# Gathered rows in a ring of eight slots, added in pairs on VectorE

## What is computed

```python
def _L0_rec_ref(user_rep, indices, item_embeddings, W_fuse, b_fuse, W_proj, b_proj):
    retrieved = jnp.mean(item_embeddings[indices], axis=1)
    fused_input = jnp.concatenate([user_rep, retrieved], axis=1)
    fused_rep = fused_input @ W_fuse + b_fuse
    logits = fused_rep @ W_proj + b_proj
    return logits
```

## Time and profile before

| what | value |
|---|---|
| median of 3 runs | 384.41 us (383.92 to 385.25) |
| profiled execution, span from first to last instruction | 381.9 us |
| PE busy | 334.2 us, 88% |
| DVE busy | 164.6 us, 43% |
| ACT busy | 75.0 us, 20% |
| POOL busy | 119.1 us, 31% |
| moved by DMA | 79.97 MB, 209 GB/s over the span |
| granted TensorE clock, mean | 0.945 of full speed |

### The profile page before, as it was taken

How to read it: one execution, slowest core, us unless ns; L and a number is a source line. 1 busy time by engine, 2 the same in 40 slices (tenths; PEclk the granted TensorE clock), 3 DMA queues, 4 the chain that set the end, 5 groups by cost and what they waited for, 6 DMA issues and landing times.

```text
span 381.9 us, 5012 instructions
## 1 busy us (share of the span) xinstructions
PE 334.2 (88%) x1420; PEld 263.3 (69%) x1420; DVE 164.6 (43%) x334; ACT 75.0 (20%) x134; POOL 119.1 (31%) x99
## 2 busy tenths in 40 slices
PE   2579069868997998399999999999999999999996
PEld 2233056545885886188888888888888888888885
DVE  3682236436724321424444445454535454545322
ACT  2220026332400200025123121122121212210000
POOL 2877878787878887200000000000000000000000
PEclk9999559968999899689999999999999999999999
DMA  7898899999999999944687767676666767642222
GB/s 237 234 171 154 172 380 270 262 233 369 264 255 224 232 183 203 214 181 154 195 246 226 228 212 217 212 213 202 217 204 215 220 210 218 211 161 88 100 88 99
DMA packets 44208, 79.97 MB, mean 209 GB/s; under 512 B 5913, under 2 KB 33697, under 8 KB 44194
## 3 DMA queue, kind: packets, MB, share of 16 engines
q1 hardware_dynamic: 32370, 56.74, 45.7%
q0 software_dynamic: 10240, 20.98, 28.8%
q10 hardware_dynamic: 1584, 2.10, 1.6%
HBM read 54.19 MB, written 25.60 MB: 209 GB/s over the span
## 4 chain that ended last, share of the span: by engine, by line
PE 57%; POOL 17%; DMA 13%; issue 10%; POOLq 1%; DVE 1%; DVEq 0%
PE bank L645 55%; POOL acc L302 17%; DMA acc<-L_rec_item_embeddings,rows 7%; DMA acc<-L_rec_item_embeddings,lap_rows 4%; DMA idx<-r_indices 1%; PE bank L632 1%; POOLq L323 1%; POOLq L72 0%; PE bank L622 0%; POOL lap_rows L329 0%; DVE acc L493 0%; DVE out_sb L507 0%; POOLq L324 0%; DVE out_sb L450 0%; DVE out_sb L452 0%
## 5 line engine op out<-in xcount | busy, mean ns | idle before, releaser
L645 PE MATMUL bank<-w_hi,f_hi 128*128 (+1 forms) x400 | 159.7, 399 | 6.3 <-DVE out_sb L507 6.3
L645 PE MATMUL bank<-w_lo,f_hi 128*128 (+1 forms) x400 | 158.1, 395 | 0.0
L645 PE MATMUL bank<-w_hi,f_lo 128*128 (+1 forms) x400 | 157.5, 394 | 0.0
L507 DVE TENSOR_TENSOR out_sb<-bank,early 128x500 f32<-128x500 f32 x100 | 67.8, 678 | 146.0 <-PE bank L645 117.5
L645 PEld LDWEIGHTS bank<-w_hi,f_hi 128*128 128x128 f32 x400 | 76.8, 192 | 27.7 <-DVE out_sb L507 7.2
L348 ACT CAST w_hi<-w_raw 128x500 f32 (+1 forms) x100 | 59.5, 610 | 145.4 <-DMA w_raw<-L_rec_W_proj 135.8
L645 PEld LDWEIGHTS bank<-w_hi,f_lo 128*128 128x128 f32 x400 | 76.8, 192 | 16.0
L645 PEld LDWEIGHTS bank<-w_lo,f_hi 128*128 128x128 f32 x400 | 76.9, 192 | 15.0
L425 DVE TENSOR_TENSOR w_lo<-w_raw,w_hi 128x500 fp32r<-128x500 f32 (+1 forms) x100 | 66.3, 672 | 21.4 <-ACT w_hi L348 20.1
L302 POOL DMA_INDIRECT acc<-L_rec_item_embeddings,lap_rows x40 | 64.4, 1610 | 17.0 <-issue 7.9
L302 POOL DMA_INDIRECT acc<-L_rec_item_embeddings,rows x40 | 52.1, 1302 | 18.9 <-issue 11.7
(11 more groups left out here) (41 smaller groups left out, 63.9 us busy)
## 6 DMA issues: line engine op xcount, KB each, us to landing
w_raw<-L_rec_W_proj SPq DMA_DIRECT2D x100, 250.0 KB
logits<-out_sb SPq DMA_DIRECT2D x100, 250.0 KB
early<-L_rec_b_proj SPq DMA_DIRECT2D x17, 250.0 KB, 3.8
acc<-r_user_rep ACTq DMA_DIRECT2D x1, 1024.0 KB, 6.0
early<-L_rec_W_fuse ACTq DMA_DIRECT2D x1, 1024.0 KB
wf_ret<-L_rec_W_fuse SPq DMA_DIRECT2D x4, 256.0 KB
acc<-L_rec_item_embeddings,rows POOLq DMA_INDIRECT x40
acc<-L_rec_item_embeddings,lap_rows POOLq DMA_INDIRECT x40
```

The source lines that it names most:

```text
L507: nc.vector.tensor_tensor(out_sb[:, slot:slot + 1, :], ps[:, 0:CHUNK].unsqueeze(1), bias[:, bass.ds(bias_slot, 1), 0:CHUNK], ALU.add).then ...
L645: m = nc.tensor.matmul(ps[:, 0:CHUNK].unsqueeze(1), f[:, t, k, :], w, start=first, stop=(f is f_lo and k == HK - 1))
```

## The change

The function is rewritten; what it does in the parts that matter:

- A tile's 20 columns are 18 plain gathers into `ring` (8 slots of a row, shared by the tiles and used round and round: gather i of tile t takes slot (18 t + i) mod 8), one plain gather into `home`, and one accumulating gather onto `home` from a loop with a count that is data. The loop runs once here. Over four tiles that is 76 plain gathers and 4 accumulating ones (before 20 and 60).
- DVE adds the ring in pairs (`add_pair`, 1024 elements a partition) into `total`, adds `home`, then the halves of `total`. Of tile 0, DVE adds seven pairs of the nine, the first two of them in one instruction; PE adds the last four slots and `total` by matmuls against the identity that accumulate in PSUM (`sum_in`).
- POOL waits in `place_free` until DVE (or PE) has read the slot that it gathers into.
- The last row enters as a bias of `mean` on ACT (`last_mean`), not by an addition of 512 elements on DVE. `mean` is four instructions, and `fuse` has its loops exchanged, so that each quarter of `ret_t` is used as it comes.
- The host hands over user_rep transposed, the indices in tile order and the last row as columns. PE's 16 transposes of user_rep, ACT's four copies after them and the spreading of the last row are gone.
- W_proj is loaded and split in halves of a chunk (1000 elements a partition) in place of quarters (500): half as many issues on SP and half as many instructions on ACT and DVE, each with twice the elements.
- SP issues the loads of chunks 0 and 1 and of wf_ret at the start, without waits on gathers; the first indices come as a transfer of their own.
- Sorting stops after 24 of 50 columns, three rounds in place of seven.
- Phase 1 uses three PSUM banks in place of two, and all tiles store out of four slots of `out_sb` in rotation.

```diff
+            def place_free(t, i):
+                q = PASSING * t + i - RING
+                if q < 0:
+                    return
+                u, j = q // PASSING, q % PASSING
+                if j >= 2 * pairs(u):
+                    pool.wait_ge(slot_summed, j - 2 * pairs(u) + 1)
+                else:
+                    pool.wait_ge(added, adds_done(u, max(1, j // 2)))
...
             for t in range(TILES):
...
-                for s in range(ACC_SLOTS):
-                    pool.wait_ge(gathered[t][s], 16)
-                    gather(t, s, rows[:, t, ACC_SLOTS + s:ACC_SLOTS + s + 1], compute_op=ALU.add)\
-                        .then_inc(gathered[t][s], 16)
...
+                for i in range(PASSING):
...
+                    if i == HOME_AT:
...
+                        gather_home(t)
+                    if i == LAPS_AT:
+                        more_laps(t)
+                    place_free(t, i)
+                    gather(ring[:, place(t, i), :], rows[:, t, i:i + 1]).then_inc(slot_landed[place(t, i)], 16)
...
+            def add_pair(t, j):
+                if j == 1:
+                    if t == 1:
+                        dve.wait_ge(slot_summed, PE_SLOTS)
+                    elif t:
+                        dve.wait_ge(ret_turned, t - 1)
+                    wait_pair(t, 0)
+                    before = pair(t, 0)
+                else:
+                    dve.wait_ge(added, adds_done(t, j - 1))
+                    before = total[:]
+                wait_pair(t, j)
+                nc.vector.tensor_tensor(total[:], before, pair(t, j), ALU.add).then_inc(added, 1)
...
+            for c in range(RESIDENT):
+                add_pair(1, c + 1)
+                if c < 4:
+                    split_lo(c + 4)
+                evacuate(0, c)
+                if c == 5:
+                    sort(3)
+            add_home(1)
+            add_halves(1)
+            fused_lo(1)
             for t in range(1, TILES - 1):
...
+                for c in range(RESIDENT):
+                    if c < 4:
+                        add_pair(t + 1, 2 * c + 1)
+                        add_pair(t + 1, 2 * c + 2)
+                    elif c == 4:
+                        add_home(t + 1)
+                    elif c == 5:
+                        add_halves(t + 1)
+                    elif c == 7:
+                        fused_lo(t + 1)
+                    evacuate(t, c)
```

819 lines of the change are left out of this document (393 added, 426 removed).

## The result

| what | before | after |
|---|---|---|
| median | 384.75 us (4 runs) | 378.28 us (4 runs, 377.36 to 380.12) |
| ratio, 95% interval | | 0.9845 (0.9813 to 0.9878) |
| span of the profiled execution | 381.9 us | 378.3 us |
| behind the last sum | 219.4 us | 217.9 us |
| POOL busy | 119.1 us | 98.4 us |

The change gains 6.5 us, 1.6%. The forecast was 13.5 us, 3.5%. The profiled execution was the slowest of the four: 378.3 of span, 380.12 of time. Against the predicted span of 368.3 it is 10.0 us late. Its time is 1.8 us above its span, where the forecast had added 2.5.

What follows compares the result with a forecast made beforehand. The prediction took gathers to bound the kernel until tile 3's sum, then PE alone: that sum at 148.9 us plus 219.4 gives a span of 368.3, plus 2.5 gives 371 us, 13.5 less; range 360 to 389.

Steps and rivals of the forecast that it cites:

- behind the last sum: From tile 3's last sum to the span's end, PE alone runs 924 matmuls; the forecast kept this at 219.4 us.
- the predicted span of 368.3: Whole kernel: tile 3's sum ready at 148.9 us plus the unchanged 219.4 us behind it.
- the forecast had added 2.5: Step from profiled span to measured time: before, median 384.41 against span 381.9, so 2.5 us was added, giving 371.
- an average share of busy time: POOL's gathers beside DVE: two-input work in 40% of the time loses 0.24 us a gather, pitch 1.5 for 1.26.
- the mean load: DMA up to 149 us: 39 MB, 262 GB/s, against 396 GB/s moved with plain gathers and loads, so room on the mean.
- the price of a landing: Time from a plain gather's start until its rows land: 4.3 us taken, with 3.4 and 7.0 as ends.

## What to carry to other kernels

Where a buffer ring ties a fast engine to a slow one, look at what stands ahead of the consumer's first instruction on its own engine: moving three additions ahead of evacuations was worth more here (8.2 us on one chip) than all the faster gathers (6.5). Price contention by the longest row of instructions without a gap as well as by an average share of busy time. Place loads that nobody needs yet behind the transfer that is on the path, even if the mean load is far below the limit. Take the price of a landing from the gather that stands on the path. And time the unchanged kernel beside every set of variants: a part that no edit touched differed by 4 to 5 us between sets.
